# One table for rotary factors, identity and mask in a transformer kernel's start

## The reference, cut to what matters

```python
def apply_rope(x):                       # on queries and keys, heads of 128
    phase = pos[:, None] * inv_freq[None, :]
    phase = jnp.tile(phase, (1, 2))[None, :, None, :]
    return (x * jnp.cos(phase) + rotate_half(x) * jnp.sin(phase)).astype(x.dtype)

q = apply_rope((layernorm(x) @ Wq).reshape(b, t, 32, 128))
k = apply_rope((ctx @ Wk).reshape(b, t, 8, 128))
v = (ctx @ Wv).reshape(b, t, 8, 128)
logits = 30 * tanh(einsum(q, k) * 0.0883 / 30)
logits = jnp.where(mask, logits, -1e+30)  # mask: one 64 x 64 pattern for all
x = x + (softmax(logits) @ v) @ Wo
```

## Time and profile before

| what | us |
|---|---|
| median of 3 runs (lowest, highest) | 850.9 (850.83, 851.1) |
| the profiled execution | 851.64 |
| its span | 849.8 |
| PE busy in the span | 837.1 |
| DVE, ACT, POOL busy | 522.7, 370.6, 345.8 |
| ACT's three small loads issued at | 0.72, 1.16, 1.64 |

### The profile page before, as it was taken

How to read it: one execution, slowest core, us unless ns; L and a number is a source line. 1 busy time by engine, 2 the same in 40 slices (tenths; PEclk the granted TensorE clock), 3 DMA queues, 4 the chain that set the end, 5 groups by cost and what they waited for, 6 DMA issues and landing times.

```text
span 849.8 us, 12526 instructions
## 1 busy us (share of the span) xinstructions
PE 837.1 (98%) x4694; PEld 695.5 (82%) x4694; DVE 522.7 (62%) x997; ACT 370.6 (44%) x923; POOL 345.8 (41%) x271
## 2 busy tenths in 40 slices
PE   6999999999999999999999999999999999999998
PEld 5888888888888888888877778898888888888776
DVE  5956655655655655655666537455366667677894
ACT  5443222222122222222223143567787877777742
POOL 4777544644543643543545440112232431233322
PEclk9999999999999999999999999999999999999999
DMA  8122310410310410310311122011010210300002
GB/s 302 51 63 64 99 38 28 123 39 25 100 38 25 125 39 24 100 40 18 104 42 42 53 81 82 13 39 50 13 38 26 55 33 14 124 13 1 1 1 99
DMA packets 24892, 48.15 MB, mean 57 GB/s; under 512 B 3584, under 2 KB 4736, under 8 KB 24704
## 3 DMA queue, kind: packets, MB, share of 16 engines
q1 hardware_dynamic: 24400, 47.22, 18.8%
q10 hardware_dynamic: 432, 0.14, 0.1%
HBM read 45.12 MB, written 2.23 MB: 56 GB/s over the span
## 4 chain that ended last, share of the span: by engine, by line
PE 93%; ACT 2%; POOL 2%; DVE 2%; DMA 1%; issue 1%; SPq 0%; POOLq 0%; DVEq 0%
PE PB L1222 24%; PE PB L1224 23%; PE PB L1223 23%; PE PB L1381 8%; PE PB L1312 4%; PE PB L1286 3%; PE PB L1396 3%; PE PB L1229 3%; PE PB L1296 1%; PE PB L1333 1%; DMA arena<-in_ctxT 1%; PE PB L1435 1%; POOL qb L782 1%; PE PB L1347 0%; POOL WQl L759 0%
## 5 line engine op out<-in xcount | busy, mean ns | idle before, releaser
L782 POOL TENSOR_TENSOR qb<-qb,arena 128x512 f32<-128x512 f32 x64 | 83.7, 1308 | 151.4 <-DVE arena L1085 151.4
L1007 DVE TENSOR_TENSOR xs<-xs,PB 128x512 f32<-128x512 f32 x112 | 76.7, 686 | 99.2 <-PE PB L1224 91.1
L846 ACT ACTIVATE Oh<-PB 96x128 fp32r<-96x128 f32 (+2 forms) x236 | 79.4, 360 | 60.4 <-PE PB L1312 37.3
L1222 PE MATMUL PB<-WOh,Oh 128*128 128x512 f32 x242 | 94.5, 390 | 0.0
L1224 PE MATMUL PB<-WOh,Ol 128*128 128x512 f32 x242 | 94.2, 389 | 0.0
L1223 PE MATMUL PB<-WOl,Oh 128*128 128x512 f32 x242 | 94.2, 389 | 0.0
L1082 DVE TENSOR_TENSOR qb<-PB,ropeq 128x512 f32<-128x512 f32 x64 | 44.2, 691 | 69.4 <-PE PB L1224 68.4
L846 ACT ACTIVATE WOh<-stage 128x512 fp32r<-128x512 f32 (+1 forms) x32 | 19.5, 620 | 132.6 <-PE PB L1224 132.6
L1222 PE MATMUL PB<-xTh,WQh 128*128 128x512 f32 x192 | 76.5, 399 | 0.0
L1224 PE MATMUL PB<-xTh,WQl 128*128 128x512 f32 x192 | 74.9, 390 | 0.0
L759 POOL TENSOR_TENSOR WQl<-stage,WQh 128x512 fp32r<-128x512 f32 x38 | 48.9, 1289 | 63.6 <-ACT WQh L846 62.9
(11 more groups left out here) (240 smaller groups left out, 2166.5 us busy)
## 6 DMA issues: line engine op xcount, KB each, us to landing
stage<-in_wq SPq DMA_DIRECT2D x44, 256.0 KB, 2.8
stage<-in_wo SPq DMA_DIRECT2D x44, 256.0 KB, 2.7
arena<-recs SPq DMA_DIRECT2D x32, 256.0 KB, 3.8
stage<-in_wk SPq DMA_DIRECT2D x13, 256.0 KB, 2.7
arena<-in_ctxT SPq DMA_DIRECT2D x8, 256.0 KB, 5.4
stage<-in_wv SPq DMA_DIRECT2D x8, 256.0 KB, 3.5
xs<-in_x SPq DMA_DIRECT2D x8, 256.0 KB, 6.1
out<-xs SPq DMA_DIRECT2D x8, 256.0 KB, 2.0
```

Of the source, the lines that this page charges most:

```text
L782: e.tensor_tensor(dst, dst, tmp, ALU.add).then_inc(s_radd)
L846: return e.activation(dst, src, ACT.Copy)
L1007: e.tensor_tensor(xs[:, i, :], xs[:, i, :], PB[b][:, :], ALU.add).then_inc(free[b])
L1222: e.matmul(dst, Ah, Bh, start=(k == 0), stop=False)
```

## The change

Rotary table, identity and mask become columns of one array `tab` of 128 x 272 f32 (0 to 127 rotary, 128 to 255 identity, 256 to 271 the mask's bytes), loaded with one DMA under one semaphore, `s_tab`, in place of three. ACT issued the three at the head of its program; the one is issued in a step `tab_load` behind the splits of the value weights. The mask steps of DVE, PE and POOL leave the start of the list and become one step `many` behind the first three value tiles, and the product takes the ring's next bank in place of bank 3. The small buffers `many`, `mv` and `sm` move in the on-chip memory; nothing else changes its size.

```diff
     step("load", "wk0", 0)
     step("consts")
-    tile("many", bank=3)
     step("ctx_load", 0)
...
     split("wk0", 0)
-    step("mask_tables")
     step("ctx", 0)
     for c in range(2):
         split("wv0", 0, c)
+    step("tab_load")
     step("ctx_load", 1)
...
     stage("k0", 0, 0)
     for i in range(3):
         stage("v0", 0, i)
+    stage("many")
     step("wk0_split")
     step("v0_move", 0, 0)
...
-        rope = sb("rope", [128, 2, 64])
+        tab = sb("tab", [128, 272])
+        rope = tab[:, 0:128].rearrange("p (a n) -> p a n", a=2)
+        ident = tab[:, 128:256]
+        mask8 = tab[:, 256:272].bitcast(u8)
...
-                if kind == "consts":
-                    e.dma_start(mask32[:, :], a["mask"]).then_inc(s_mask, 16)
-                    e.dma_start(rope[:, :, :], a["rope"].rearrange("p (a n) -> p a n", a=2)).then_inc(s_rope, 16)
-                    e.dma_start(ident[:, :], a["ident"]).then_inc(s_ident, 16)
+                if kind == "tab_load":
+                    e.dma_start(tab[:, :], a["tab"]).then_inc(s_tab, 16)
...
-                if kind == "consts":
-                    dve.wait_ge(s_mask, 16)
-                    e.tensor_copy(keep[:, :], mask8).then_inc(s_mb)
-                elif kind == "ctx":
+                if kind == "ctx":
...
-                    dve.wait_ge(s_rope, 16)
+                    dve.wait_ge(s_tab, 16)
                     dve.wait_ge(*done(kind, *k))
...
-                elif kind == "mask_tables":
+                elif kind == "many":
+                    b = bank_of("many")
+                    dve.wait_ge(s_tab, 16)
+                    e.tensor_copy(keep[:, :], mask8).then_inc(s_mb)
                     dve.wait_ge(*done("many"))
-                    e.tensor_scalar(many[:, :], PT[:, 0:64], 1.0, None, ALU.min).then_inc(free[3])
+                    e.tensor_scalar(many[:, :], PB[b][:, 0:64], 1.0, None, ALU.min).then_inc(free[b])
...
-                    pe.wait_ge(s_ident, 16)
+                    pe.wait_ge(s_tab, 16)
...
-                elif kind == "mask_tables":
+                elif kind == "many":
                     pe.wait_ge(s_one, 1)
                     pe.wait_ge(s_mb, 1)
-                    e.matmul(PT[:, 0:64], pTb[:, 0, 0:128], keep[:, :], start=True, stop=True).then_inc(full[3])
+                    e.matmul(PB[b][:, 0:64], pTb[:, 0, 0:128], keep[:, :], start=True, stop=True).then_inc(full[b])
```

More of the change, by code:

```diff
@@ L3 @@
 from contextlib import ExitStack
-INS = ["x", "ctxT", "mask", "rope", "ident", "lowtri", "wq0", "wk0", "wv0", "wo0", "aw", "bcat",
+INS = ["x", "ctxT", "tab", "lowtri", "wq0", "wk0", "wv0", "wo0", "aw", "bcat",
        "wq1", "wk1", "wv1", "wo1", "w1", "a1", "bf1", "coef", "scl", "bias"]
@@ L485, in program @@
         rec = sb("rec", [128, 2, 128])
-        rope = sb("rope", [128, 2, 64])
+        tab = sb("tab", [128, 272])
+        rope = tab[:, 0:128].rearrange("p (a n) -> p a n", a=2)
+        ident = tab[:, 128:256]
+        mask8 = tab[:, 256:272].bitcast(u8)
         keep = sb("keep", [128, 64])
         ones = sb("ones", [128, 32])
+        many = sb("many", [128, 64])
+        mv = sb("mv", [128, 8, 2])
+        sm = sb("sm", [128, 2, 2, 8])
         xs = sb("xs", [128, 8, 512])
@@ L534, in program @@
         V1l = sb("V1l", [128, 2, 2, 2, 96], f32r)
[L535 to L538, removed]
         ropeq = sb("ropeq", [128, 2, 64])
@@ L544, in program @@
         st6 = sb("st6", [128, 8, 6])
-        mv = sb("mv", [128, 8, 2])
         lnb = sb("lnb", [128, 5, 8])
-        sm = sb("sm", [128, 2, 2, 8])
         wk0_1 = qb[:, 1, 0:512]
@@ L583, in program @@
         s_ldx = [sem(f"ld_x{i}") for i in range(8)]
-        s_ident, s_rope, s_mask = sem("ld_ident"), sem("ld_rope"), sem("ld_mask")
+        s_tab = sem("ld_tab")
         s_aw, s_bcat, s_low = sem("ld_aw"), sem("ld_bcat"), sem("ld_lowtri")
@@ L759, in gpsimd_program @@
                     e.tensor_tensor(lo, staged[:, n % 4, 0:cols], hi.bitcast(f32), ALU.subtract).then_inc(s_wlo)
-                elif kind == "mask_tables":
-                    pool.wait_ge(s_rope, 16)
+                elif kind == "many":
+                    pool.wait_ge(s_tab, 16)
                     pool.wait_ge(*read("many"))
@@ L1232, in tensor_program @@
             for kind, *k in steps:
-                if kind in ("k0", "q0", "v0", "e0", "sum0", "xT", "k1", "v1", "b1", "c1", "e1", "weff",
+                if kind in ("k0", "q0", "v0", "e0", "sum0", "xT", "many", "k1", "v1", "b1", "c1", "e1", "weff",
                             "dense", "mgT", "delta"):
@@ L1488 @@
         "ctxT": g["ctx_4096"].reshape(1024, 512).T,
-        "mask": np.ascontiguousarray(np.concatenate([g["mask_1x1xSxS2_bk0"].reshape(64, 64).T] * 2, 0)).view(np.int32),
-        "rope": rope.astype(np.float32),
-        "ident": np.eye(128, dtype=np.float32),
+        "tab": np.concatenate([rope.astype(np.float32), np.eye(128, dtype=np.float32), np.ascontiguousarray(
+            np.concatenate([g["mask_1x1xSxS2_bk0"].reshape(64, 64).T] * 2, 0)).view(np.float32)], 1),
         "lowtri": np.broadcast_to(low, (128, 16)),
```

## The result

| | before | changed |
|---|---|---|
| median of 9 timed runs each, us | 850.82 | 853.08 |
| lowest to highest | 850.43 to 851.1 | 852.84 to 853.49 |
| profiled execution (span) | 851.64 (849.8) | 853.08 (851.3) |

The changed kernel is slower by 2.26 us: ratio 1.0028, 95% interval 1.0019 to 1.0036. The forecast was 852.4; the direction and the places of the waits were right, the size was forecast too small (1.5), and the result lies beyond the 0.2% that I had set as the border to no change.

The account below looks back on a forecast made before the run. PE was taken to bound the kernel, its losses before 45 us lasting to the end. Front -0.5, product, ACT's order and bank +2.0, table and later waits 0: +1.5 on 850.9, so 852.4 us; 8-in-10 range 851.0 to 853.5.

Parts of the forecast that it names:

- What bounds the kernel: Whole kernel: PE is busy 837.1 of 849.8 us; every microsecond it loses before 45 us is missing at the end.
- Rival 2: After 45 us: PE's later waits absorb the delay, or ACT moves sooner; 850.4 to 851.4 us, chance 0.12.
- Product: Mask product behind three value tiles waits for DVE's copy, starts at 18.65 in old times; PE stands 0.7 us.
- queue behind it: ACT's fixed order after the first transposes: third x tile at 19.35, value tile 2's move ending 23.1 to 23.2.
- bank: Second key tile gets value tile 2's bank, waits for ACT's move: 23.2 in old times, 22.7 shifted, 1.5 us late.
- GpSimd's split: Second key weight's split after the mask steps ends at 22.5, 22.0 shifted; covered by ACT's move, late next without the bank.
- Front -0.5: Start of the kernel: without three loads heading ACT's queue, context and x land 0.5 us earlier.
- +2.0: Up to the second key tile: product, ACT's order and bank together add 2.0 us, 0.8 of it the product.
- Table late (1): Before k0's rotation: table lands late, 852.8 to 853.8 us; or no front gain, 852.9; chance 0.25 for either.
- Clock (3): PE's value tiles: without the early product the clock rises 2 us later, costing 1.0 us; 852.65 us, chance 0.05.
- GpSimd alone (4): Second key tile: front gains more, bank is no wait, GpSimd's 22.0 decides; +0.8, 851.7 us, chance 0.13.
- The chance of slower than 0.2% (0.36): Whole time: chance 0.36 of measuring slower than the no-change band of 849.2 to 852.6 us.

Follow-up runs that it names:

- e1_bank3: The changed kernel with the mask product back in bank 3, outside the ring, nothing else changed; 852.17 us, ratio to before 1.0013.
- e10_head_extra: The changed kernel with the table's load at the head of ACT's queue and three more copies of it behind; 854.06 us, ratio to before 1.0035.
- e4_bank3_pool: The changed kernel with the product in bank 3 and GpSimd's mask steps behind two weight splits; 851.91 us, ratio to before 1.0009.

## Why the prediction was right in its steps and short in its sum

**What bounds the kernel: right.** Every profile has the same 830.4 us, within 0.2, from the start of the second key tile on; what is lost before it stays lost. Rival 2, that the delay is taken up later, is out.

**Product, queue behind it, bank: right.** In the time frame of the first profile of before (S at 10.57), forecast and then measured (S + 8.09, 8.34, 8.98 and 12.77): product 18.65, 18.66; first transposes 18.7, 18.91; third x tile 19.35, 19.55; key tile 23.2, 23.34. The product held PE for 0.25, not 0.05 to 0.1. PE's wait before it was put at 0.4 to 0.8; it was 1.47 in the first profile and 0.55 in the second, where the faster pace came late as in the rows that the forecast used. GpSimd's split was late next as said, by experiment.

**The sum: two terms mis-sized.** First, "Front -0.5": x did land 0.67 earlier in the first pair of profiles, but the timed runs give the table's place at most 0.3 and, by their medians, nothing. By the medians S is 9.9 and 10.1 in the changed kernel and, with 10.55 to 10.66 of distance, 9.8 to 10.15 in before. I took the time that q10's packets held the engines as time won for q1. Its share did grow, from 79.7 to 88.2%, but with fewer bytes (0.76 to 0.72 MB): its packets only took longer. The other profiles say the same. From 3 to 6 us q1 moved 0.76, 0.80 and 0.76 MB at 79.7 to 80.6% in the three with three loads at the head of ACT's program, and 0.70 to 0.84 MB at 88.2 to 102.6%, by the profile's count, in the seven with none. And my first profile had x late for this kernel (S 10.57), so that the 0.67 between the two first profiles is mostly this chance. It is also why the key tile's start was forecast to 0.03: x came 0.17 earlier than forecast, and the distance was 0.14 longer; in the second profile the tile stood at 23.02. Second, "+2.0": it is 12.77 - 10.55 = 2.2. About 0.1 is the product and the splits behind it, and 0.1 is the profile of before that I counted from, in which the clock came up late and the key tile stood at 10.66. With 0 and 2.2 the sum is 2.2; measured 2.26.

**How the 2.2 divides: half right.** I gave 0.8 to the product and 1.2 to bank and ACT's order, and nothing to GpSimd's split, which I took to be hidden behind ACT's move. In the changed kernel it is hidden, and its own time was forecast well: 22.5, which is 11.93 after S, against 11.68 and 11.77 where it decides. But the two shares can't be read off as costs, because the waits cover each other. Taken back alone, the copy's place gives 1.00 and the bank 1.09, both down to GpSimd's split; bank and GpSimd's steps together give 1.26 (12.77 to 11.51), the copy on top of them another 0.87, in all 12.77 - 10.64 = 2.13. While the other two waits stand, GpSimd's steps cost nothing that shows; with both gone they would delay the tile by about 1.0 to 1.1 (11.68 or 11.77 against 10.64), an estimate, since that run was not made.

**The rivals.** Table late (1): no, it landed 1.4 before its use; its second half, that the front gives nothing, is what the timed runs show within 0.3, and its 852.9 was the nearest figure. Clock (3): the faster pace was there from 12.2 and 14.5 us in the two profiles of the changed kernel and from 12.5 and 14.7 in those of before, whatever stands at 3.99, and moved neither kernel's distance by more than 0.11. GpSimd alone (4): not in the changed kernel; with the bank taken back (e1_bank3, 852.17) GpSimd did decide, at the 22.5 of the forecast's old times, less 0.25. The chance of slower than 0.2% (0.36) came out low because I placed the front's gain at a single profile's value.

## What to carry to other kernels

A step put into a ring of buffers changes not only its own wait but who waits for whom behind it: list for each later tile which one it now follows, and when that one is emptied. On an in-order engine a product is as late as the slowest step ahead of the copy that feeds it, here a rotation that it did not need. When several waits end at the same tile, taking back one shows only how far the next one lies behind it; what a wait is worth shows when the others are gone. And a gain of half a microsecond read from the transfers of one execution is no term of a sum until a second execution shows that the landing is stable.

## What the runs showed of the hardware that I had not expected

- The landing of x moved by 0.35 and 0.45 us between two profiles of one kernel (9.90 and 10.25; 10.57 and 10.12), more than the place of a 136 KB load does (0.2 to 0.3 at most). Over the seven profiles that have no load at the head of ACT's program S lies between 9.66 and 10.25.
- PE's step from 1.2 to 2.4 GHz (products with 256 columns issue 0.21, then 0.12 apart) came by 12.5 us in one profile of before and at 14.7 in the other; the windows' granted clock reads 1.00 all the while. The earliest is in e10_head_extra, at 11.1 us, where products with 512 columns go from 0.43 to 0.24 apart:

```profile
10.68 0.59 PE L1225 MATMUL PB<-cTl,WKh 128*128 128x512 f32 x1
11.10 0.40 PE L1226 MATMUL PB<-cTh,WKl 128*128 128x512 f32 x1
11.34 0.40 PE L1224 MATMUL PB<-cTh,WKh 128*128 128x512 f32 x1
```
- GpSimd's `many` step of 128x64 took 0.24 where DVE was idle (19.54 above), and 0.56 in the kernel before, where DVE worked beside it on two operands in the on-chip memory. Below are that step and DVE's first low-part subtraction in the kernel before; the step ended 0.10 after the subtraction, and in the second profile of before 0.09 after it. DVE being busy is not enough for that: in e4_bank3_pool the step took 0.24 (at 22.10) while DVE subtracted all the time, there with one operand in PSUM. That this operand makes the difference is not tested by itself:

```profile
6.03 0.56 POOL L766 TENSOR_SCALAR many<-many 128x64 f32<-128x64 f32 x1
```
```profile
5.56 0.93 DVE L1019 TENSOR_TENSOR cTl<-arena,cTh 128x512 fp32r<-128x512 f32 x1 [0.66 <-ACT cTh L846]
```
```profile
22.10 0.24 POOL L769 TENSOR_SCALAR many<-many 128x64 f32<-128x64 f32 x1
```
```profile
21.46 1.89 DVE L1057 TENSOR_TENSOR xTl<-PB,xTh 128x512 fp32r<-128x512 f32 x3 [0.49 <-ACT xTh L849]
```

- DVE's subtraction took 0.93 in the kernel before, beside GpSimd's mask steps, 1.02 in the changed kernel, beside GpSimd's split of the first key weight (4.17 to 5.43), and 0.69 at 7.07 there, where GpSimd stood idle:

```profile
4.97 1.02 DVE L1015 TENSOR_TENSOR cTl<-arena,cTh 128x512 fp32r<-128x512 f32 x1 [4.97 <-ACT cTh L847]
7.07 0.69 DVE L1015 TENSOR_TENSOR cTl<-arena,cTh 128x512 fp32r<-128x512 f32 x1 [1.09 <-ACT cTh L847]
```
